# A two-layer gated cross-attention model on one core: loads, warm-ups and router scores at the seams, the order of causal jobs, and seven rooms of maxima in the lead-in

## The reference, cut to what matters

```python
x = x + tanh(g_xattn[0]) * L0_xattn(layernorm(x), ctx)
x = x + tanh(g_ffn[0])   * L0_ffn(layernorm(x))        # k = 256 tokens per expert
x = x + tanh(g_xattn[1]) * L1_xattn(layernorm(x), ctx, ctx)
x = x + tanh(g_ffn[1])   * L1_ffn(layernorm(x))        # k = 512 tokens per expert

def L0_xattn(x, ctx):
    y  = softmax(causal(heads(x@Wq+bq) @ heads(x@Wk+bk).T / sqrt(32))) @ heads(x@Wv+bv)
    y += softmax(heads(x@Wcq+bcq) @ heads(ctx@Wck+bck).T / sqrt(32)) @ heads(ctx@Wcv+bcv)
    return y @ Wp + bp
def L1_xattn(q, k, v):                                  # cross attention alone
    return softmax(heads(q@Wq+bq) @ heads(k@Wk+bk).T / sqrt(32)) @ heads(v@Wv+bv) @ Wo + bo
def ffn(x):                                             # 8 experts, each picks its top k tokens
    probs = softmax(x @ Ws + bs).T
    vals, routes = top_k(probs, k)
    h = gelu(x[routes] @ W1 + b1)
    return scatter_add(routes, (h @ W2 + b2) * vals)
```

## Time and profile before

| | us |
|---|---|
| median of 3 runs | 3955.64 (3955.27 to 3960.52) |
| the profiled execution | 3960.93 |
| its span | 3959.2 |
| TensorE busy | 3770.1 (95% of the span), mean granted clock 0.978 |
| proj0 | 13 to 418 |
| attn0, out0, route0 | 419.5 to 1585, to 1675, to 1730 |
| experts0, proj1 | to 2118, to 2202 |
| attn1, out1, route1 | to 3070, to 3149, to 3206 |
| experts1 | to 3959.2 |

### The profile page before, as it was taken

The page is one execution under the profiler, slowest core; times in us unless marked ns, Lnnn a source line. Parts: engine busy times, 40 slices in busy tenths (PEclk is TensorE's granted clock), DMA queues, the critical chain, the costliest instruction groups (busy, mean ns, idle before and its releaser), DMA issues. The chain is left out here.

```text
span 3959.2 us, 76116 instructions
## 1 busy us (share of the span) xinstructions
PE 3770.1 (95%) x30798; PEld 2638.8 (67%) x30798; DVE 2524.3 (64%) x2907; ACT 2081.3 (53%) x3667; POOL 1774.6 (45%) x876
## 2 busy tenths in 40 slices
PE   7999799999999999889998799999999889999998
PEld 6777466666666665669996455555555658888886
DVE  4444688878788885776664677777775763343442
ACT  3222266666666666256662366666666344344442
POOL 0000287687678768001210488888888011111110
PEclk9999799999999999899998899999999899999999
DMA  7666724424433440646665323223220534434341
GB/s 231 226 223 221 197 62 107 110 70 102 107 98 82 100 100 19 234 142 203 214 206 154 112 76 78 78 76 80 77 55 28 207 100 119 119 109 119 109 117 37
DMA packets 289363, 485.27 MB, mean 123 GB/s; under 512 B 23088, under 2 KB 120880, under 8 KB 287024
## 3 DMA queue, kind: packets, MB, share of 16 engines
q1 hardware_dynamic: 272784, 440.39, 37.4%
q0 software_dynamic: 14752, 40.38, 4.4%
q10 hardware_dynamic: 1536, 0.40, 0.1%
HBM read 350.67 MB, written 130.02 MB: 121 GB/s over the span
## 5 line engine op out<-in xcount | busy, mean ns | idle before, releaser
L957 ACT ACTIVATE attn_probs<-attn_low 128x512 f32<-128x512 f32 (+1 forms) x2368 | 1234.7, 595 | 463.7 <-PE attn_low L867 345.7
L998 DVE TENSOR_REDUCE attn_parts<-attn_mx 128x4 f32<-128x2048 f32 x538 | 1232.8, 2291 | 364.6 <-PE attn_mx L839 359.3
L816 POOL TENSOR_TENSOR attn_psums<-attn_psums,attn_probs 128x1024 f32<-128x1024 f32 x536 | 1275.1, 2379 | 66.3 <-ACT attn_probs L957 0.8
L867 PE MATMUL attn_low<-attn_queries,attn_keys 97*128 97x256 f32 x3072 | 580.3, 309 | 4.2 <-ACT attn_probs L957 4.0
L867 PEld LDWEIGHTS attn_low<-attn_queries,attn_keys 97*128 97x128 f32 x3072 | 416.0, 188 | 235.2 <-ACT attn_probs L957 124.6
L1746 DVE TENSOR_TENSOR ring_low<-ring_raw,ring_high 128x2048 fp32r<-128x2048 f32 x124 | 284.3, 2293 | 202.4 <-ACT ring_high L1704 202.4
L884 PE MATMUL attn_low<-attn_probs,attn_values 128*32 128x256 f32 x6144 | 411.1, 385 | 1.4 <-ACT attn_probs L957 1.4
L813 POOL TENSOR_TENSOR attn_psums<-attn_probs 128x1024 f32<-128x1024 f32 x88 | 209.7, 2383 | 371.8 <-ACT attn_probs L957 371.8
L1660 PE MATMUL ffn_up<-ffn_xH,ring_high 128*128 128x256 f32 (+1 forms) x1024 | 348.1, 340 | 2.7 <-DVE ffn_xL L1752 2.7
L1660 PE MATMUL ffn_up<-ffn_xH,ring_low 128*128 128x256 f32 (+1 forms) x1024 | 348.6, 340 | 0.0
L1660 PE MATMUL ffn_up<-ffn_xL,ring_high 128*128 128x256 f32 (+1 forms) x1024 | 347.5, 339 | 0.0
(11 more groups left out here) (216 smaller groups left out, 5438.0 us busy)
## 6 DMA issues: line engine op xcount, KB each, us to landing
ring_raw<-in_L_ffn_W_dram SPq DMA_DIRECT2D x128, 1024.0 KB, 5.4
attn_keys<-l_cross_keys SPq DMA_DIRECT2D x72, 512.0 KB, 7.3
attn_queries<-l_queries SPq DMA_DIRECT2D x48, 512.0 KB, 4.8
l_cross_keys<-proj_high SPq DMA_DIRECT2D x64, 256.0 KB, 2.5
l_cross_keys<-proj_lowp SPq DMA_DIRECT2D x64, 256.0 KB, 3.1
l_cross_values<-proj_vout SPq DMA_DIRECT2D x64, 256.0 KB, 3.3
lent_keys<-l_keys SPq DMA_DIRECT2D x48, 256.0 KB, 3.7
attn_keysn<-l_cross_keys SPq DMA_DIRECT2D x12, 1024.0 KB, 5.0
```

The source lines that it names most:

```text
L816: pool.tensor_tensor(ps, ps, at, ALU.add).then_inc(added, 1)
L867: mm = pe.matmul(out[:, n0:], KS[b][0:3 * HD + 1, h, kb * P:(kb + 1) * P], QS[b][0:3 * HD + 1, h, job.qb * QB + n0:(job.qb + 1) * QB], sta ...
L957: act.activation(probs[:, m % RING, i // 2, heads, n0:], sc[:, item % SC, :].rearrange("p (h q) -> p h q", q=QB)[:, :, n0:], ACT.Exp, scal ...
L998: op = dve.tensor_reduce(into, seen, AX.X, ALU.max)
```

## The change

It does these things:

- The eight bias loads of proj0 are issued by proj0's block, not the constants' block. ScalarE and VectorE wait for a source's biases ahead of its first evacuation. GpSimd's first token load waits for the early weights.
- In proj1 the lent keys are loaded once the weight is there, the values in two halves later, and attn1's first queries, into buffers that are now lent as well (`take_queries`), once they are stored.
- All `busy` matmuls of the projections, the lead-ins and the out stages are gone.
- Causal units take their jobs in the order qb = 3, 2, 1, 0. The lead-in holds no more groups than the first two jobs have: seven in layer 0, eleven before. In layer 1 it is eleven as before.
- The router scores of four tiles are computed at once, transposed: four products, one for each 128 of the width, into four stripes of 32 partitions of one bank; ScalarE copies it, and a product with a selector per tile adds up the stripes.
- The expert blocks end without GpSimd's drain.

```diff
@@ Projections.begin, and project, SyncE
         for w in early:
             self.load_weight(sp, w)
-        for w in self.weights:
-            self.load_bias(sp, w)
...
             if not begun:
                 st.begin(sp, early)
+            for w in weights:
+                st.load_bias(sp, w)
             if lent is not None:
+                for w in early:
+                    sp.wait_ge(st.raw_in[w], DMA)
                 lent.load_keys(sp, unit)
             for g, (s, b, j) in enumerate(plan.at):
+                if lent is not None and g in (1, G - 1):
+                    lent.load_values(sp, unit, int(g > 1))
+                if lent is not None and b and j == 0:
+                    last = plan.rows[g - 1, unit.row]
+                    sp.wait_ge(row_out[last % RING], 2 * DMA * (last // RING + 1))
+                    lent.load_queries(sp, unit)
@@ project, GpSimd, TensorE, ScalarE (VectorE has the same lines as ScalarE)
+            if not begun:
+                for w in early:
+                    pool.wait_ge(st.raw_in[w], DMA)
             for g in range(1, G):
...
-            busy(pe, c, bank[0][:, :], 28 if begun else 36)
             turn_tokens(0)
...
-            for s in range(len(sources)):
-                act.wait_ge(st.bias_in[s], DMA * len(sources[s].outs))
             for g, (s, _, _) in enumerate(plan.at):
+                if s not in [x for x, _, _ in plan.at[:g]]:
+                    act.wait_ge(st.bias_in[s], DMA * len(sources[s].outs))
@@ Plan
-            for qb in range(T // QB):
-                self.jobs.append(Job(unit, u, qb, n))
+            order = range(T // QB)[::-1] if unit.causal else range(T // QB)
+            for qb in order:
+                self.jobs.append(Job(unit, u, qb, n, qb == order[0]))
...
         lead = max(g - x for g, x in enumerate(due[:24]))
-        while done < lead:
+        while done < min(lead, self.groups_before[2]):
             self.place(done, -1)
@@ Lent
+    def take_queries(self, ph):
+
+        self.QS = ph.sb("queries0", [P, GH, T], F32R)
+        self.QN = ph.sb("queriesn0", [P, T], F32R)
...
+    def load_queries(self, sp, unit):
+
+        sp.dma_start(self.QN[:, :].bitcast(F32), unit.q_src[unit.row, :, 0, :]).then_inc(self.flat_in, DMA)
+        for row, half in enumerate((0, 0, 1)):
+            sp.dma_start(self.QS[row * HD:(row + 1) * HD, :, :].bitcast(F32),
+                         unit.q_src[unit.row, :, half, :].rearrange("(h d) n -> d h n", d=HD)
                          ).then_inc(self.stack_in, DMA)
@@ attention: SyncE; TensorE, maxima and the end of the lead-in
-                for piece in range(FLAT):
-                    if piece or not lent.early:
+                if not lent.early:
+                    for piece in range(FLAT):
                         load_flat(sp, 0, piece)
-                for piece in range(STACK):
-                    if 6 <= piece < 9 or not lent.early:
+                    for piece in range(STACK):
                         load_stack(sp, 0, piece)
...
-                    if job.qb == 0 and g == 0:
+                    if job.head and g == 0:
                         pe.wait_ge(flat_in[b], FLAT * DMA * (job.u // BUFS + 1))
...
-                    if 1 < k < LEADS:
-                        busy(pe, c, room[:, 0, :], 3)
...
                 pe.wait_ge(max_read, LEADS // 2 * 2)
-                busy(pe, c, low[:, SC, :], 3)
@@ out_stage: GpSimd and SyncE; TensorE; ScalarE; VectorE
+                pool.memset(wr[:, :, :], 0.0).then_inc(wr_cleared, 1)
...
-                sp.dma_start(wr[:, :, :], w_router.rearrange("(c p) n -> p c n", p=P)).then_inc(wr_in, DMA)
+                sp.wait_ge(wr_cleared, 1)
+                sp.dma_start(wr[:, :, 0:E], w_router.rearrange("(c p) n -> p c n", p=P)).then_inc(wr_in, DMA)
...
-                def scores(t):
-                    if t == 0:
+                def scores(i):
+                    if i == 0:
                         pe.wait_ge(wr_in, DMA * (1 if b_router is None else 2))
-                    pe.wait_ge(xT_ready, t + 1)
+                    pe.wait_ge(xT_ready, (i + 1) * TB)
+                    if i:
+                        pe.wait_ge(kept, i)
                     for ch in range(C):
-                        mm = pe.matmul(lg[:, t, :], xT[t % 2][:, ch, :], wr[:, ch, :], start=ch == 0, stop=ch == C - 1)
+                        mm = pe.matmul(lgT[ch * P // C:(ch + 1) * P // C, :], wr[:, ch, :], xT[i % 2][:, ch, :],
+                                       start=True, stop=True)
+                    mm.then_inc(scored, 1)
+
+                def collect(i):
+                    if i == 0:
+                        pe.wait_ge(sel_ready, 1)
+                    pe.wait_ge(kept, i + 1)
+                    for t in range(i * TB, (i + 1) * TB):
+                        mm = pe.matmul(lg[:, t, :], partial[:, t % TB * P:(t % TB + 1) * P], sel[:, :],
+                                       start=True, stop=True)
                     mm.then_inc(routed, 1)
 
-                busy(pe, c, bank[3][:, :], 9)
                 for t in range(TILES + 2):
                     if t < TILES:
                         products(t)
                     if t >= 2:
                         turns(t - 2)
-                    if t >= 3:
-                        scores(t - 3)
-                scores(TILES - 1)
+                    if t >= 3 and (t - 3) % TB == TB - 1:
+                        scores((t - 3) // TB)
+                    if t >= 4 and (t - 4) % TB == TB - 1:
+                        collect((t - 4) // TB)
+                scores(BLOCKS - 1)
+                collect(BLOCKS - 1)
...
+                def keep(i):
+                    act.wait_ge(scored, i + 1)
+                    if i:
+                        act.wait_ge(routed, i)
+                    act.activation(partial[:, :], lgT[:, :], ACT.Copy).then_inc(kept, 1)
...
+                dve.tensor_reduce(sel[:, :], c["ident"][:, :].rearrange("p (c m) -> p m c", c=C)[:, 0:E, :], AX.X, ALU.add
+                                  ).then_inc(sel_ready, 1)
@@ experts
-        with nc.Block() as block:
+        with nc.Block(no_gpsimd_drain=True) as block:
```

More of the change, by code:

```diff
@@ L457, in _ @@
             turned_low(0)
-            for s in range(len(sources)):
-                dve.wait_ge(st.bias_in[s], DMA * len(sources[s].outs))
             for g, (s, _, _) in enumerate(plan.at):
+                if s not in [x for x, _, _ in plan.at[:g]]:
+                    dve.wait_ge(st.bias_in[s], DMA * len(sources[s].outs))
                 for k, (n, t) in enumerate(sources[s].units):
@@ L657, in load_keys, with load_values @@
                              ).then_inc(self.stack_in, DMA)
[L658 to L661 removed]
+    def load_queries(self, sp, unit):
[3 more added lines that the diff above has]
+                         unit.q_src[unit.row, :, half, :].rearrange("(h d) n -> d h n", d=HD)
+                         ).then_inc(self.stack_in, DMA)
+    def load_values(self, sp, unit, half):
+        n = unit.keys // 2
+        k0 = half * n
+        sp.dma_start(self.VS[:, k0 // P:(k0 + n) // P, :],
+                     unit.v_src[unit.row, k0:k0 + n, :].rearrange("(t p) f -> p t f", p=P)
+                     ).then_inc(self.stack_in, DMA)
     def load_out(self, sp, y, w_out):
@@ L1833, in program @@
             lent = Lent(ph, c, "lent0", False)
-            attention(nc, "attn0", c,
-                      [unit for u in range(UNITS)
-                       for unit in (Unit(T, True, queries, keys, values, y_self, u),
-                                    Unit(TC, False, cross_queries, cross_keys, cross_values, y_cross, u))],
-                      lent, (y_self, L0_xattn_Wp))
+            with Phase(nc, "lentq0") as ph:
+                lent.take_queries(ph)
+                attention(nc, "attn0", c,
+                          [unit for u in range(UNITS)
+                           for unit in (Unit(T, True, queries, keys, values, y_self, u),
+                                        Unit(TC, False, cross_queries, cross_keys, cross_values, y_cross, u))],
+                          lent, (y_self, L0_xattn_Wp))
             out_stage(nc, "out0", c, lent, (y_self, y_cross), L0_xattn_Wp, L0_xattn_bp, c["tanhg"][:, 0:1], x, x1, xn1,
```

47 lines of the change are left out of this document (28 added, 19 removed).

## The result

The changed kernel takes 3949.91 us (median, 3946.34 to 3959.78) against 3959.61 (3952.67 to 3964.23) for the kernel before, run beside it. The ratio is 0.9979, 95% interval 0.9972 to 0.9987: 8.3 us, with 5 to 11 in the interval. The forecast was 15.8. The profiled execution has a span of 3947.8 us, 11.4 less than before.

What follows compares the result with a forecast made beforehand. TensorE, busy 95% of the span, was taken as the bound, so gains come from the seams: 9.0 + 1.0 + 0 + 3.8 + 2.8 + 0.5 − 1.3 = 15.8 off 3955.6, giving 3940 us, range 3928 to 3952.

Steps and rivals of the forecast that it cites:

- Term 1: Program start: biases behind the constants' block and no warm-ups bring the first product to about 12.5; +9.0 us.
- Term 2: Layer 0's attention lead-in: scores start 13.7 us earlier, four groups moved into steps cost 12.7; net +1.
- Rival A: Layer 0's lead-in and double steps: clock stays low without warm-ups, term 2 falls to −7; 3948 us, chance 0.18.
- Term 3: Causal units of attention: reversed job order only turns the same steps round; 0, give or take 2 us.
- rival C: Causal units: crowded job ends make VectorE late, say 2.4 us a unit, 19 over eight; 3959 us, chance 0.05.
- Term 4: Out stages: router scores transposed by block save TensorE time, mostly in the second stage; +3.8 us (0 to +7).
- Terms 5 and 6: Second projection's first product sooner, +2.8 us; second attention's lead-in, nearly all hidden behind the fence copy, +0.5.
- Term 7: Ends of expert stages: GpSimd's drain moves into the next barrier, 0; three new barrier rounds cost −1.3 us.

Runs made afterwards that it cites:

- e3: The changed kernel with the warm-up matmuls of both attention lead-ins put back; 3957.64 us, ratio 0.9992 to the kernel before.
- e10: The kernel before with only causal jobs longest first and the cap of seven groups in layer 0's lead-in; 3964.61 us, ratio 1.0014.
- e4: The changed kernel with a double step's second group put behind the values of the step before; 3944.94 us, ratio 0.996 to the kernel before.
- e9: e4 with longest job first in the first causal unit alone, shortest first in the other seven; 3943.36 us, ratio 0.9954 to the kernel before.
- e11: The kernel before without the warm-up matmuls of the two attention lead-ins, nothing else changed; 3955.39 us, ratio 0.9985.
- e1: The changed kernel with causal jobs shortest first and no cap, so eleven groups in the lead-in; 3942.34 us, ratio 0.9952 to the kernel before.
- e12: e1 with the lead-ins' warm-up matmuls put back; 3946.97 us, ratio 0.9964 to the kernel before.
- e8: e2 with longest job first in the first causal unit alone, shortest first in the other seven; 3942.92 us, ratio 0.9961 to the kernel before.
- e6: The kernel before with the changed out stage alone; 3964.57 us, ratio 1.0006.
- e13: e1 with the out stage of the kernel before, its nine warm-ups included; 3943.64 us, ratio 0.9959 to the kernel before.
- e7: The changed kernel with GpSimd's drain put back at the end of both expert stages; 3954.13 us, ratio 0.9981 to the kernel before.
- e2: The changed kernel without the cap: eleven groups in the lead-in, longest job first; 3944.40 us, ratio 0.9957 to the kernel before.

## Why the prediction was wrong, and what of it held

**Term 1, the start: right.** Expected +9.0 and a first product at 12.5; it was at 12.55, and 9.6 in the trace, 7.9 as a kernel of its own. ScalarE's and VectorE's chain ran as worked out.

**Term 2, the lead-in: this step failed.** It had +13.7 less 12.7, so +1 net; the traces of before and after have +13.1 less 15.5, so −2.4. The failed step is the price of moving four groups into the steps. For the four double steps themselves it was right: from the first scores to the fifth step's first exponential the changed kernel takes 35.4 and the kernel before 22.7, which is the 12.7. What was left out is what follows: the next six steps took 22.5 in place of 19.7, since the clock fell again at 463.1 (they took 20.5 in e3 and e10, where it did not); the other 0.8 is not explained. The wait in series is a large part of a double step's price: with the second group behind the values (e4, e9) the four take 27.4 and 28.4, though the clock has a share in that. And the sum compared with the wrong kernel. Its 13.7 was taken against a lead-in with warm-ups, 3.8 of which goes with them (e11); against e1, eleven groups without warm-ups, the cap saves 9.5 and the ten steps cost 14.5 more, so −5.1.

Rival A's condition came true, its price did not: the clock was low for 51 us and again from 463.1, through three double steps and most of the fourth, and term 2 is −2.4 and not −7. Part of each double step is VectorE's two reduces, 2.29 each at either clock, and the low clock adds nothing to them. The Trainium skill (TensorE: Matmul & The Clock Gate, Why this matters for your kernels) advises against idle gaps between bursts. The traces of e3 and e10 agree in kind: with warm-ups the ten steps' low-clock cost is 9.8 and 10.3 and not 13.4. But the totals are 5 to 8 us longer with warm-ups in three comparisons by medians, so the measurement decides against filling the gaps here.

**A term that was missing: the lead-ins' warm-ups.** I had given them 0.9 in attn1 and a risk. Their removal is worth about 5 (e11; e12 agrees). It was luck for the number that this gain, which the sum doesn't have, hid part of the job part's loss. The row that showed it was in the trace of before: VectorE idle for 2.58 ahead of a group whose matmuls stood behind warm-ups.

**Term 3, the order: size wrong.** Expected 0 with 2 either way, measured −2.4 in the body (0.2 to 0.3 a pair). The crowded ends of rival C are seen in the rows above, at about a tenth of its price. e8 and e9 show it by undoing it in seven of eight units.

**Term 4, the out stages.** Expected +3.8; the traces give +2.5 to +5.5 in out1 and about nothing in out0, which fits. By ratio e6 has −2.4, and the new stage is worth +2.8 between e13 and e1, within noise; they do not confirm it, and it stays open.

**Terms 5 and 6.** Expected +2.8 and +0.5; measured +2.6 and −0.3 in the trace. The copy and the memset hid the queries, as written.

**Term 7.** Right in the main: the drain moved, 4951 ns long, and e7 is level. Two more barrier rounds are seen on GpSimd's list (21 in place of 19), not three.

**The sum.** 15.8 less 3.4 for term 2 and 2.4 for term 3 is 10.0, near the 11.4 of the two spans and inside the interval of the ratio, whose middle is 8.3. By totals the parts are the start +8, the lead-ins' warm-ups +5, and the job part −5 (e10) to −11 (e1 against the changed kernel, by ratios), where terms 2 and 3 had +1. That leaves 0 to 6 for the rest; the totals are too noisy to say more.

One sentence of the description of the change was wrong: GpSimd's wait for the early weights ahead of its first token load stands in proj1, not in proj0, where GpSimd issues that load at 8.26 us. No term rested on it.

## What to carry to other kernels

When work is taken out of a lead-in and put into steady steps, price it at the wait it adds to the bounding engine's queue, and put it where other work of that engine stands between its two halves: four steps with a second group took 35.4 us back to back and 27.4 and 28.4 with it behind the values, 23.7 in e1 without one. Take each term's price against the kernel that has the other parts of the change already. Warm-up matmuls stand in a queue like any others; before keeping or removing them look at who is idle behind them. And look at the low clock's cost when stages are compared: in eight kernels with the same attn1 (the changed kernel's) it was 8.7 to 13.3 us there.

## What the runs showed of the hardware

- TensorE's granted clock stayed at 0.50 from 408.5 to 459.7 in the changed kernel, and rose at 456.6 in e2 and 455.4 in e4, all without warm-ups. With seven groups, warm-ups broke the low stretch up (e3: full speed at 430.3 to 433.7, 450.8 to 454.2 and 461.1 to 464.5). With eleven they bought nothing: from proj0's end to the first cross scores the low-clock cost was 9.6 to 15.4 in four kernels without them and 12.6 to 18.9 in four with them, the warm-ups' own time included.
- Low-clock cost of a whole program, by the traces, was 44.8 (e2) to 66.5 us (e6); I see no relation to what was changed. Single stretches of low clock fell into steady work too (e1 at 631 us, e6 at 2734), and TensorE was busy through them.
- The copy of 128 x 128 on VectorE beside GpSimd's memset took 6.20 to 6.56 us in each kernel, in both attentions.
